# First expert of a top-2 expert layer: its first product started on the tokens of three chunks, the low halves of its weights made by column quarters

## The reference

```python
x = x + tanh(g_xattn) * attention(layernorm(x), ctx, ctx)
x = x + tanh(g_ffn) * ffn(layernorm(x))

def ffn(x):                     # N = 4096 tokens, 8 experts, 2 per token
    probs = softmax(x @ Wr + br)
    gates, ids = top_k(probs, 2)
    # each expert takes its cap = ceil(1.2 * N / 8) = 615 tokens of largest gate
    h = silu(xg @ W1[e] + b1[e])        # 615 x 512 by 512 x 2048
    out = h @ W2[e] + b2[e]             # 615 x 2048 by 2048 x 512
    y[token] += gate * out
```

## Time and profile before

| | |
|---|---|
| Median of 3 runs | 1789.11 us |
| Lowest, highest | 1787.97, 1789.23 us |
| Profiled execution | 1788.94 us, of which 1787.2 us span |
| TensorE matmul busy | 1698.6 us (95%) |
| VectorE busy | 1056.1 us (59%) |
| ScalarE busy | 799.5 us (45%) |
| GpSimd busy | 540.7 us (30%) |
| TensorE's granted clock, mean | 0.98 |
| First product of expert 0 starts | 949.06 us |

### The profile page before, as it was taken

How to read it: one execution, slowest core, us unless ns; L and a number is a source line. 1 busy time by engine, 2 the same in 40 slices (tenths; PEclk the granted TensorE clock), 3 DMA queues, 4 the chain that set the end, 5 groups by cost and what they waited for, 6 DMA issues and landing times.

```text
span 1787.2 us, 29087 instructions
## 1 busy us (share of the span) xinstructions
PE 1698.6 (95%) x10115; PEld 826.5 (46%) x10115; DVE 1056.1 (59%) x2083; ACT 799.5 (45%) x1093; POOL 540.7 (30%) x524
## 2 busy tenths in 40 slices
PE   7999999999999999999719999999999999999997
PEld 4324243332424334242206556474655647465563
DVE  6768867687786868767686525254352625434331
ACT  4563736446373654636314425162442516244240
POOL 2353635435363543626201211211111121111101
PEclk9999999999999999999859999999999999999999
DMA  6334263443425343432203634536263452626312
GB/s 222 115 66 147 73 174 109 115 137 83 150 80 161 122 108 124 97 98 94 110 33 113 175 78 134 145 100 165 52 178 71 142 137 100 162 63 177 70 38 29
DMA packets 214606, 203.17 MB, mean 114 GB/s; under 512 B 121812, under 2 KB 162912, under 8 KB 210456
## 3 DMA queue, kind: packets, MB, share of 16 engines
q1 hardware_dynamic: 193432, 181.80, 33.7%
q0 software_dynamic: 21120, 20.67, 6.7%
HBM read 134.57 MB, written 43.63 MB: 100 GB/s over the span
## 4 chain that ended last, share of the span: by engine, by line
PE 77%; DVE 13%; issue 4%; POOL 2%; DMA 1%; ACT 1%; SPq 1%; DVEq 0%; POOLq 0%; ACTq 0%
PE psum L1643 23%; PE psum L1619 21%; PE psum L1380 6%; PE psum L1409 5%; PE psum L1390 5%; PE psum L1507 5%; DVE mx L969 5%; PE psum L1424 4%; PE psum L1400 4%; PE psum L1435 2%; POOL pt L628 1%; DVE reached L1132 1%; DVE x2hl L1052 1%; DVE x2hl L1054 1%; SPq L489 1%
## 5 line engine op out<-in xcount | busy, mean ns | idle before, releaser
L1643 PE MATMUL psum<-w,hT 128*128 128x512 f16 (+1 forms) x1920 | 415.7, 379 | 0.0
L1619 PE MATMUL psum<-xgT,w 128*128 128x308 f16 (+1 forms) x3072 | 408.1, 293 | 0.5 <-DVE xgT L1233 0.5
L969 DVE TENSOR_REDUCE mx<-psum 128x1 f32<-128x512 f32 x512 | 327.7, 686 | 90.8 <-PE psum L1390 88.4
L1619 PEld LDWEIGHTS psum<-xgT,w 128*128 128x128 f16 x3072 | 296.1, 97 | 109.4 <-DVE xgT L1233 0.9
L1643 PEld LDWEIGHTS psum<-w,hT 128*128 128x128 f16 (+1 forms) x1920 | 199.3, 104 | 213.8
L895 ACT ACTIVATE h<-psum,b1c 128x308 f32<-128x308 f32 (+1 forms) x256 | 118.0, 512 | 340.8 <-PE psum L1619 340.3
L704 POOL DMA_INDIRECT out_dram<-y,idx_now x40 | 87.3, 2184 | 499.0 <-DVE y L1286 312.4
L1254 DVE TENSOR_TENSOR hT<-h,hT 128x615 f16<-128x615 f32 x128 | 102.5, 801 | 210.2 <-ACT hT L898 210.2
L1283 DVE SCALAR_TENSOR_TENSOR y<-psum,b2b 128x512 f32<-128x512 f32 (+1 forms) x40 | 27.7, 692 | 270.2 <-PE psum L1643 270.2
L1390 PE MATMUL psum<-stk 96*128 96x512 f16 x512 | 171.8, 383 | 10.5 <-DVE mx L969 1.5
L1380 PE MATMUL psum<-actT,wT 128*128 128x512 f16 x768 | 179.2, 381 | 2.0 <-DVE wT L956 2.0
(11 more groups left out here) (218 smaller groups left out, 1805.9 us busy)
## 6 DMA issues: line engine op xcount, KB each, us to landing
stage<-in_L_ffn_W_dram SPq DMA_DIRECT2D x62, 1024.0 KB, 5.3
stk<-qk_rows SPq DMA_DIRECT2D x192, 128.0 KB, 2.6
qk_rows<-qks SPq DMA_DIRECT2D x64, 256.0 KB, 2.6
xin<-in_x_dram SPq DMA_DIRECT2D x8, 1024.0 KB, 5.4
cin<-in_ctx_dram SPq DMA_DIRECT2D x8, 1024.0 KB, 7.5
xres<-in_x_dram SPq DMA_DIRECT2D x8, 1024.0 KB, 5.6
out_dram<-xres SPq DMA_DIRECT2D x32, 256.0 KB, 2.2
x_split<-x2hl SPq DMA_DIRECT2D x32, 256.0 KB, 2.3
```

Of the source, the lines that this page charges most:

```text
L969: v.reduce_max(mx[:, KT * t + qt:KT * t + qt + 1], ps, AX.X).then_inc(read, 1)
L1619: mm = t_.matmul(psum[:, (2 * m + ch) % 4, 0:c1 - c0], w1[:, wp, kt, m * P:(m + 1) * P], xgT[:, KT * xp + kt, c0:c1], start=(kt == 0 and ( ...
L1643: mm = t_.matmul(psum[0:rows, Y_BANK[i], :], hT[:, hp, k, c * P:c * P + rows], w2[:, wp, k, :], start=(k == 0 and (hp, wp) == (0, 0)), sto ...
```

## The change

Four things are changed, all at the start of expert 0. VectorE makes the low quarters by column quarters (quarter 0 of all four row chunks, then quarter 1, and so on) and does all five copies of turned tokens behind column quarter 0. TensorE turns chunks 0 to 2, runs the first column half of block 0, turns chunks 3 and 4, runs the first half of block 1, then the second halves of blocks 0 and 1; three pairs of `keep_busy` matmuls are gone. Block 0 of expert 0 waits for the four quarters of column quarter 0, and blocks 4, 8 and 12 for those of theirs. ScalarE waits for the halves in the order in which they are now finished. SP waits for all 16 low quarters ahead of W2's chunks 0 and 1 (before: 12 and 16).

```diff
+FIRST_CHUNKS = (tuple(range(C)), (), (), ())
+FIRST_H = ((0, 0), (1, 0), (0, 1), (1, 1))
...
-                    sp.wait_ge(chunk_split, 4 * n - 4)
+                    sp.wait_ge(chunk_split, 16 if isinstance(n, int) and n in (4, 5) else 4 * n - 4)
...
-                        act.wait_ge(h_full, 2 * MT * e + 2 * m + ch + 1)
+                        order = FIRST_H.index((m, ch)) if isinstance(e, int) and e == 0 and m < 2 else 2 * m + ch
+                        act.wait_ge(h_full, 2 * MT * e + order + 1)
...
-                if q == 0:
-                    dve.wait_ge(chunk_hi, i + 1)
+                dve.wait_ge(chunk_hi, i + 1)
...
-            for i in range(4):
-                for q in range(4):
+            for q in range(4):
+                for i in range(4):
                     first_lo(i, q)
-                    if i >= 2 and q % 2 == 1:
-                        copy_chunk(2 * (i - 2) + q // 2)
-            copy_chunk(C - 1)
+                for c in FIRST_CHUNKS[q]:
+                    copy_chunk(c)
...
+            def hidden(e, m, chs, lows):
+
+                for kt in range(KT):
+                    if lows:
+                        pe.wait_ge(chunk_split, m + kt + 1 if isinstance(e, int) and e == 0 else 4 * (8 * e + kt + 1))
+                    for wp, xp in PARTS:
+                        for ch in chs:
...
+            pe.wait_ge(chunk_hi, 1)
+            keep_busy(8)
+            for c in range(3):
+                turn_chunk(c)
+                if c < 2:
+                    keep_busy(2)
+            pe.wait_ge(xgT_read, 3)
+            hidden(0, 0, (0,), True)
+            for c in range(3, C):
+                turn_chunk(c)
+            hidden(0, 1, (0,), False)
+            pe.wait_ge(xgT_read, C)
+            for m in range(2):
+                hidden(0, m, (1,), False)
...
+                for m in range(2 if first else 0, MT):
...
+                    hidden(e, m, (0, 1), m == 0 or (first and m % 4 == 0))
```

More of the change, by code:

```diff
@@ L1588, in keep_busy, with turn_chunk @@
                     t_.matmul(psum[:, 4, :], w1[:, 0, 0, 0:P], w1[:, 0, 0, 0:512], start=True, stop=True)
-            pe.wait_ge(chunk_hi, 1)
-            keep_busy(8)
-            for c in range(C):
+            def turn_chunk(c):
                 pe.wait_ge(xg_first[c], 16)
@@ L1598, in _ @@
                 last.then_inc(xgT_full, 1)
-                keep_busy(2)
+            def hidden(e, m, chs, lows):
[4 more added lines that the diff above has]
+                        for ch in chs:
+                            c0, c1 = CHUNKS[ch]
+                            mm = t_.matmul(psum[:, (2 * m + ch) % 4, 0:c1 - c0], w1[:, wp, kt, m * P:(m + 1) * P],
+                                           xgT[:, KT * xp + kt, c0:c1], start=(kt == 0 and (wp, xp) == (0, 0)),
+                                           stop=(kt == KT - 1 and (wp, xp) == (1, 0)))
+                            if kt == KT - 1 and (wp, xp) == (1, 0):
+                                mm.then_inc(h_full, 1)
+            pe.wait_ge(chunk_hi, 1)
[12 more added lines that the diff above has]
+                hidden(0, m, (1,), False)
             def expert(e, last):
-                for m in range(MT):
+                first = isinstance(e, int) and e == 0
+                for m in range(2 if first else 0, MT):
                     if m == 0:
[L1604 to L1607, removed]
+                        pe.wait_ge(xgT_in, 16 * C * e)
                     for ch in range(2):
```

## The result

The changed kernel takes 1797.56 us (median of 5, 1797.02 to 1799.20), the kernel before 1788.91 us on the same chip (1787.86 to 1789.23). The ratio is 1.005 with a 95% interval of 1.0039 to 1.0061: slower by 8.7 us. 1797.6 us was forecast.

What follows compares the result with a forecast made beforehand. TensorE, busy 95% of the span, was taken as the bound, its start of expert 0 waiting for VectorE. Block 3's delay of 6.6 plus 2.0 us of clock made 8.6 us, from 1789.11 to 1797.6 us; range 1795.0 to 1800.8.

Steps and rivals of the forecast that it cites:

- The start of the first product: TensorE, start of expert 0: the first product starts near 946.05 instead of 949.06, 3.0 us earlier at most.
- The delay of block 3: TensorE in expert 0: block 3 starts at 965.2 instead of 958.6, +6.6 us, after standing idle 8.65 us.
- The clock: TensorE after the idle time: work at half clock for 3.7 to 4.4 us costs +2.0 us.
- The last addition: Forecast total: 8.6 us on top of the runs' median of 1789.11 us, given as 1797.6 us.
- Rival A: W2 load of expert 0 is not on the path, block 3 starts at 956.55: 1787.5 us; chance 0.05.
- B: TensorE's clock does not fall or comes back at once, only the wait is paid: 1795.5 us; chance 0.08.
- C: TensorE's clock stays low longer, costing up to 4.4 us instead of 2.0: 1800.0 us; chance 0.12.
- the early halves gain nothing here: TensorE, blocks 0 to 2 of expert 0: the 2.1 us gained is eaten inside the wait ahead of block 3.

Runs made afterwards that it cites:

- by_rows: Changed kernel with VectorE finishing low quarters row chunk by row chunk behind the copies, SP waiting for 7 and 10 instead of 16: 1789.40 us, ratio 1.0009.
- no_early: Changed kernel with TensorE's old order: all five chunks turned with fillers, then blocks 0 and 1 with both halves together: 1795.99 us, ratio 1.0040.
- late_half: Kernel before with the first W2 load of expert 0 issued only when half of expert 1's table rows are made: 1791.73 us, ratio 1.0017.
- late_load: Kernel before with the first W2 load of expert 0 issued only when the rows of expert 1's table are made: 1796.02 us, ratio 1.0043.
- conv_late: Changed kernel with ScalarE's conversion of expert 0's first W2 quarter moved from behind block 0 to behind block 3: 1787.10 us, ratio 0.9993.
- by_rows_conv1: by_rows with ScalarE's conversion of the first W2 quarter behind block 1 instead of block 0: 1787.53 us, ratio 0.9990, two slow executions left out.
- filled: Changed kernel with 36 filler matmuls on TensorE ahead of block 3 of expert 0: 1795.79 us, ratio 1.0036.

## Why the prediction was right

The mechanism and its place were right: the load behind the wait for 16, ScalarE behind the load, TensorE behind ScalarE's reading of block 1, and the clock. The kernel before with the late load alone shows 7.4 of the 8.7 us, and moving ScalarE's conversion away takes all of it back. The total is closer than its terms deserve: block 3's delay was forecast 0.5 us too high, the clock's cost 0.9 us too low, and in the profiled execution the stages ahead of expert 0, which are outside the sum, were 1.0 us shorter. That these nearly cancel is luck.

- **The start of the first product.** Forecast 3.0 us earlier, measured 3.66 us against the slot selection (9.87 and 13.53). In the trace of before chunk 2 was turned at half clock behind fillers; and the gathers came faster (below).
- **The delay of block 3.** Forecast 6.6 us, measured 6.1: 29.2 us after the slot selection against 23.1 before. The load was issued 20.7 us after the slot selection where the forecast had 21.3, as everything ahead of it had started sooner. The idle time of 8.65 us was 8.83. The landing, 5.5 us in the sum, took 5.56.
- **The clock.** Forecast 2.0 us, from stretches at half level of 3.7 and 4.4 us; here it was 6.0 us and cost 2.9. This is the mis-sized term. The second stretch was misread: at 29.09, when work resumed, the clock was still full, and it fell only at 30.0, as the window below has it, so the work at half level lasted 3.4 us there (to 33.46), not 4.4, and cost 1.7 us.

```profile
29.00:30.00 1.00, 0.92 (x5) 0.47 (x6) 0.00 (x0) 0.00 (x0) 0.00 (x0) 1.00 0.00 0
30.00:31.00 1.00, 1.00 (x4) 0.34 (x3) 0.47 (x1) 0.00 (x0) 0.00 (x0) 0.52 1.06 178
```

  The runs show nothing (by_rows), 1.4 us (no_early, 48 matmuls in 7.89 us), 1.5 us (late_half), 1.6 us (late_load) and 2.9 us, so it is a range rather than a number. The clock fell between 2.6 us (late_half) and 5.4 us (no_early) after TensorE had stopped, and not at all in by_rows' 2.88 us. The Trainium skill (TensorE: Matmul & The Clock Gate, section on the clock gate) puts this ramp below 1% of a typical kernel's span and advises against fitting it to a count of slow matmuls. The trace agrees with the size, 2.9 us being 0.2% of this span; but it is a third of this effect, and a sum without it would have missed that.
- **The early part of the execution** was 0.97 us shorter in the profiled run. It was not in the sum and hides the difference: 6.1 and 2.9 are 9.0 us, and the span grew by 8.1.
- **The last addition.** 1789.11 + 8.6 are 1797.7, not 1797.6; nothing hangs on it.
- **Rival A** (the load is not on the path) was refuted by the rows and then built: conv_late and by_rows_conv1 are what the change would be without the stop. It gave 1787.5 us for this case; the two kernels take 1787.1 and 1787.5.
- **Rivals B and C.** B, no cost of the clock, was refuted for this stop, though by_rows shows that it can happen after a stop of 2.88 us. C, a clock at half for longer, came true in part: 2.9 us, between the forecast's 2.0 and C's 4.4.
- **That the early halves gain nothing here** was said and held: no_early is no slower.

## What to carry to other kernels

When work is reordered so that one consumer starts sooner, list every buffer that the old order freed early, and follow the transfer into it to the engine that waits for it in program order: here an unrelated conversion, standing between two steps of the critical path, turned a late load into a stop of 8.8 us. Before making such a wait shorter, try to move it: putting the waiting instruction behind the steps that TensorE needs took back all 8.7 us (conv_late), the earlier load 7.8 (by_rows). And price a stop of TensorE with its clock, as a range: here nothing to 2.9 us on top of stops of 2.8 to 8.8 us.

## What the runs showed of the hardware that I had not expected

**GpSimd's gathers took longer to issue beside VectorE's operations with two inputs.** GpSimd's timeline before, from its second gather on. VectorE makes low quarters, each from two inputs in SBUF, beside all of these but the third, which starts with a copy out of PSUM (942.31 to 943.00):

```profile
938.97 1.26 POOL L688 DMA_INDIRECT xg<-x_split,idx_new  x1 [0.30 <-issue]
940.53 1.48 POOL L688 DMA_INDIRECT xg<-x_split,idx_new  x1 [0.30 <-issue]
942.32 0.95 POOL L688 DMA_INDIRECT xg<-x_split,idx_new  x1 [0.30 <-issue]
943.57 1.44 POOL L688 DMA_INDIRECT xg<-x_split,idx_new  x1 [0.30 <-issue]
```

And in the changed kernel, where VectorE is idle or copies from 937.8 on:

```profile
938.00 0.97 POOL L690 DMA_INDIRECT xg<-x_split,idx_new  x1 [0.30 <-issue]
...
941.79 0.95 POOL L690 DMA_INDIRECT xg<-x_split,idx_new  x1 [0.31 <-issue]
```

The five issues take 6.3 us instead of 7.6 from the first start to the last end; the first takes 1.29 us in both kernels, and in both VectorE makes low quarters beside it. late_load, which has the old order of VectorE, shows 1.26, 1.48, 0.95 and 1.44 us again; no_early, with the new order, 0.94 to 0.97. The Trainium skill (SBUF — State Buffer, section on the two separate sides) says that VectorE and GpSimd share a pair of ports as an exclusive lock, and that an operation of VectorE with two inputs in SBUF takes it only against a GpSimd operation that reads SBUF. The gathers read their row numbers from SBUF (`idx_new`), and the traces agree with the page in direction and place; that it is this port and nothing else wasn't tested.

**TensorE's clock at the start of expert 0 is not the same from one execution to the next.** Around 940 to 949 us it was at half until 944.8 in the kernel before, full from 939 on in the changed one, and full and then at half from 943 to 949.9 in filled, which has the same code as the changed kernel up to block 3. In late_load, which has the same code as the kernel before up to the W2 load, it was full from 939 on. What decides it isn't shown.
